# Keys and values formed at the end of the first cross attention, two places that belong to no layer, and a deeper ring for the last gathers

## What is computed

```python
x = x + L0_xattn(layernorm(x), ctx, ctx, mask, ...)   # cross attention to 64 contexts of 257 rows
x = x + L0_attn(layernorm(x), ...)                    # delta rule over chunks, two FIR filters, gated mixture
x = x + L0_ffn(layernorm(x), W1, W2, Wr)              # 8 experts, each row goes to the best 2
x = x + L1_xattn(layernorm(x), ctx, ctx, ...)         # cross attention, 16 heads, the same contexts
x = x + L1_attn(layernorm(x), ...)                    # self attention
x = x + L1_ffn(layernorm(x), ...)                     # 16 experts, best 4, and a shared one
```

```python
k = (K @ Wk.T + bk)      # K = V = ctx: 64 x 257 x 256
v = (V @ Wv.T + bv)
```

## Times and the profile before

| | us |
|---|---|
| median of 3 runs | 1781.69 (1781.23 to 1788.0) |
| the profiled execution | 1793.83 |
| its span | 1792.0 |
| TensorE busy in it | 1591.9 (89%) |
| mean granted TensorE clock in it | 0.941 |

### The profile page before, as it was taken

One profiled execution on the slowest core, in us unless ns is written; L12 is line 12 of the kernel. 1 busy time (PEld: TensorE's weight loads), 2 busy tenths in 40 slices (PEclk: granted clock), 3 DMA queues, 4 the chain that ended last, 5 costly groups with the idle time before them and its releaser, 6 DMA issues. The chain is left out here.

```text
span 1792.0 us, 41190 instructions
## 1 busy us (share of the span) xinstructions
PE 1591.9 (89%) x16490; PEld 1215.2 (68%) x16490; DVE 1211.0 (68%) x2401; ACT 788.2 (44%) x1856; POOL 613.7 (34%) x526
## 2 busy tenths in 40 slices
PE   5986888999988959999999498999989879999998
PEld 3443366555675759999997374566668768689997
DVE  4577889680077448888881316677759867677888
ACT  1222642121133324344442234788827722476664
POOL 2330300000020066666643303587528745203210
PEclk8997989999899969999999798999989979999999
DMA  9990059401043555555538771555500000001001
GB/s 292 321 322 12 1 179 214 128 13 30 2 141 89 153 193 210 204 199 210 193 132 195 188 229 60 184 166 161 168 25 1 1 27 17 13 1 42 24 7 48
DMA packets 143213, 214.84 MB, mean 120 GB/s; under 512 B 38128, under 2 KB 116528, under 8 KB 137136
## 3 DMA queue, kind: packets, MB, share of 16 engines
q1 hardware_dynamic: 106848, 104.06, 20.2%
q0 software_dynamic: 10368, 58.47, 9.8%
q10 hardware_dynamic: 25808, 49.68, 9.5%
HBM read 164.91 MB, written 47.25 MB: 118 GB/s over the span
## 5 line engine op out<-in xcount | busy, mean ns | idle before, releaser
L286 PE MATMUL ps<-kv_ctx,kv_w 128*128 128x257 f32 x512 | 133.1, 396 | 43.2 <-PEq L1824 19.3
L2000 DVE TENSOR_TENSOR f_hL<-f_hr,f_hH 128x512 fp32r<-128x512 f32 x92 | 135.4, 1526 | 46.8 <-ACT f_hH L1951 46.7
L2158 POOL TENSOR_TENSOR a_pr<-a_pr,a_inv 128x1028 f32<-128x1028 f32 x64 | 121.6, 1900 | 72.8 <-DVE a_inv L2278 72.5
L286 PEld LDWEIGHTS ps<-kv_ctx,kv_w 128*128 128x128 f32 x512 | 94.4, 195 | 64.7 <-issue 33.9
L290 PE MATMUL ps<-kv_w,kv_ctx 128*128 128x256 f32 x512 | 124.8, 387 | 13.8 <-ACT b_kv L310 9.3
L96 PE MATMUL ps<-f_xTH,f_w1H 128*128 128x256 f32 x368 | 108.0, 293 | 18.9 <-issue 18.2
L2248 ACT ACTIVATE a_pr<-ps,a_neg 128x257 f32<-128x257 f32 x256 | 117.7, 477 | 2.6 <-DVE a_neg L2298 2.6
L290 PEld LDWEIGHTS ps<-kv_w,kv_ctx 128*128 128x128 f32 x512 | 95.1, 192 | 32.4 <-ACT b_kv L310 13.9
L1512 POOL TENSOR_TENSOR b0m_pm<-b_dr,b_gates 128x256 f32<-128x256 f32 x16 | 13.2, 830 | 296.5 <-SPq L1477 270.1
L97 PE MATMUL ps<-f_xTL,f_w1H 128*128 128x256 f32 x368 | 106.0, 288 | 0.0
L98 PE MATMUL ps<-f_xTH,f_w1L 128*128 128x256 f32 x368 | 105.9, 288 | 0.0
(11 more groups left out here) (421 smaller groups left out, 4532.0 us busy)
## 6 DMA issues: line engine op xcount, KB each, us to landing
a_kv<-kv SPq DMA_DIRECT2D x64, 513.0 KB, 3.6
a_ctxT<-in_ctxT SPq DMA_DIRECT2D x32, 514.0 KB, 7.8
a_ctxR<-in_ctx SPq DMA_DIRECT2D x32, 512.0 KB
kv<-b_kv ACTq DMA_DIRECT2D x31, 513.0 KB, 5.7
kv_ctx<-in_ctxT ACTq DMA_DIRECT2D x61, 257.0 KB, 4.0
kv<-f_raw ACTq DMA_DIRECT2D x15, 513.0 KB, 11.3
outs<-f_yo SPq DMA_DIRECT2D x23, 256.0 KB, 2.1
kv<-f0r_kv ACTq DMA_DIRECT2D x9, 513.0 KB
```

Source lines behind the costliest of these rows:

```text
L286: done = e.matmul(out[:, 0:NK], self.w[:, 0, c, cols(part)], ctx[:, c, :], start=(c == 0), stop=(c == DC - 1))
L2000: e.tensor_tensor(h[1][:, j % 2, 2 * q:2 * q + 2, :], hr[:, q, :, :], h[0][:, j % 2, 2 * q:2 * q + 2, :].bitcast(F32), ALU.subtract).then_ ...
L2158: e.tensor_tensor(pr[:, b % 3, :, :], pr[:, b % 3, :, :], inv[:, b % 2, :].unsqueeze(2).to_broadcast([P, HG, NK]), ALU.mult).then_inc(*p_p ...
```

## The change

**In the first cross attention** two batches (6 jobs) are formed behind the last outputs: TensorE runs them after its loop; ScalarE takes out four jobs ahead of the root of the next layer norm, and two behind it. Of the 64 batches the stages now form 2, 29, 9, 14 and 10. In the delta solve 14 jobs instead of 20 stand ahead of `fuse_most(0)`; the later jobs are at the places where they were, counted from the first.

**Places.** Two places, `A.own`, belong to `KeysAhead` and live through all stages, on the right side of on-chip memory. The wait for a place's store moves into `KvPlace.free`, at its next use; `A.end` is gone. Routing and queries use these two and one of their own, the experts five (two in `raw1`, the two, and one more) instead of three. `xr` is freed after the routing, so GpSimd's first load of expert weights (`gather1(0)`) now stands behind the wait for the stores from it.

**The last gathers** go into 8 places of two (one tile's pair each). A pair waits only from the ninth tile on, until VectorE has used both rows' sums of tile t - 8.

**The root** of the next layer norm at the end of the experts stands behind 36 of 42 evictions; six come after it. With the queries, 12 jobs instead of 9 stand ahead of the query product (`Q.pe`, L346).

```diff
-AHEAD = (31, 9, 15, 9)
+AHEAD = (2, 29, 9, 14, 10)
...
+class KvPlace:
...
+    def free(self, e):
+        if self.used:
+            e.wait_ge(*self.st.at(16 * self.used))
...
+        self.own = [KvPlace(Y, at, f"kv{n}") for n, at in enumerate(places(Y.sb("kv", [P, 2, KV])))]
...
-    def end(self, e):
-        many, count = len(self.kv), (self.last - self.first) // 3
-        for s in range(many):
-            e.wait_ge(*self.st[s].at(16 * ((count - s + many - 1) // many)))
...
+    A.host(AHEAD[0], (6, 7), A.own)
...
+                A.pe(e, 3 * AHEAD[0])
...
+                A.act(e, 3 * AHEAD[0] - 2)
                 K.norms["b0"].act(e)
+                A.act(e, 2)
...
-                ahead.pe(e, 20)
+                ahead.pe(e, 14)
                 fuse_most(0)
...
-                    A.act(e, 3 * AHEAD[1])
-                    A.end(e)
+                    A.act(e, 3 * AHEAD[2])
...
-        A.host(Y, AHEAD[2], (0, 1, 2, 3), places(place1[:, 0:3 * KV].rearrange("p (s n) -> p s n", s=3)))
-        yg = place2[:, 0:4 * D].rearrange("p (s n) -> p s n", s=4)
...
+        A.host(AHEAD[3], (0, 1, 2, 3), [kv2, kv3] + A.own + [kv1])
...
+                e.wait_ge(*st_r.at(16 * NT))
                 gather1(0)
-                e.wait_ge(*st_r.at(16 * NT))
...
-                for n in range(2 * NT):
-                    if n >= 4:
-                        e.wait_ge(*v_x.at(n - 3))
...
+                for t in range(NT):
+                    if t >= RING:
+                        e.wait_ge(*v_x.at(2 * (t - RING) + 2))
+                    for k in range(2):
...
-                A.act(e, 3 * AHEAD[2])
+                A.act(e, 3 * AHEAD[3] - TAIL)
                 K.norms["a1"].act(e)
-                A.end(e)
+                A.act(e, TAIL)
+                for place in (kv1, kv2, kv3):
+                    place.free(e)
...
-                    A.pe(e, 3 * AHEAD[3] - 18)
+                    A.pe(e, 3 * AHEAD[4] - 18)
                     Q.pe(e)
```

More of the change, by code:

```diff
@@ L235, in act, with __init__, store @@
             e.activation(self.raw[:, :], K.ps[:, 2, :], ACT.Copy).then_inc(*self.out.up())
+class KvPlace:
+    def __init__(self, Y, at, name):
+        self.at, self.st, self.used = at, Y.sig("dma", name), 0
+    def free(self, e):
+        if self.used:
+            e.wait_ge(*self.st.at(16 * self.used))
+    def store(self, e, out):
+        e.dma_start(out, self.at).then_inc(*self.st.up(16))
+        self.used += 1
 class KeysAhead:
@@ L252, in __init__, with host, host_of @@
         self.mm, self.ev = Y.sig("pe", "kv"), Y.sig("act", "kv")
-        self.formed = self.taken = self.first = self.last = 0
-    def host(self, Y, count, banks, kv):
-        self.first, self.last = self.last, self.last + 3 * count
-        self.banks, self.kv = banks, kv
-        self.st = [Y.sig("dma", f"kv{s}") for s in range(len(kv))]
+        self.own = [KvPlace(Y, at, f"kv{n}") for n, at in enumerate(places(Y.sb("kv", [P, 2, KV])))]
+        self.formed = self.taken = self.last = 0
+        self.hosts = []
+    def host(self, count, banks, kv):
+        self.hosts.append((self.last, banks, kv))
+        self.last += 3 * count
+    def host_of(self, j):
+        return [h for h in self.hosts if h[0] <= j][-1]
     def load(self, e, b):
@@ L275, in pe @@
             b, part = divmod(j, 3)
-            s, many = b % self.SLOTS, len(self.banks)
-            ctx, out = self.ctx[s], self.K.ps[:, self.banks[(j - self.first) % many], :]
+            first, banks, _ = self.host_of(j)
+            s, many = b % self.SLOTS, len(banks)
+            ctx, out = self.ctx[s], self.K.ps[:, banks[(j - first) % many], :]
             if j == 0:
@@ L302, in act @@
             b, part = divmod(j, 3)
-            own = b - self.first // 3
-            s = own % len(self.kv)
-            kv, src = self.kv[s], self.K.ps[:, self.banks[(j - self.first) % len(self.banks)], :]
+            first, banks, kv = self.host_of(j)
+            place = kv[(b - first // 3) % len(kv)]
+            src = self.K.ps[:, banks[(j - first) % len(banks)], :]
             e.wait_ge(*self.mm.at(j + 1))
-            if part == 0 and own >= len(self.kv):
-                e.wait_ge(*self.st[s].at(16 * (own // len(self.kv))))
+            if part == 0:
+                place.free(e)
             if part < 2:
-                done = e.activation(kv[:, cols(part, NK)], src[:, 0:NK], ACT.Identity, bias=self.bk[:, part:part + 1])
+                done = e.activation(place.at[:, cols(part, NK)], src[:, 0:NK], ACT.Identity, bias=self.bk[:, part:part + 1])
             else:
-                done = e.activation(kv[:, 2 * NK:KV], src, ACT.Copy)
+                done = e.activation(place.at[:, 2 * NK:KV], src, ACT.Copy)
             done.then_inc(*self.ev.up())
@@ L318, in act @@
                 e.wait_ge(*self.ev.at(j + 1))
-                e.dma_start(self.K.kv[b], kv).then_inc(*self.st[s].up(16))
-    def end(self, e):
-        many, count = len(self.kv), (self.last - self.first) // 3
-        for s in range(many):
-            e.wait_ge(*self.st[s].at(16 * ((count - s + many - 1) // many)))
+                place.store(e, self.K.kv[b])
 def places(t):
@@ L915, in delta_attention @@
         A = K.keys
-        A.host(Y, AHEAD[0], (6, 7), places(sb("kv", [P, 2, KV])))
+        A.host(AHEAD[1], (6, 7), A.own)
         with Layer(K, "b0a") as Z:
@@ L1325, in _ @@
                     ahead.act(e, 1)
-                ahead.act(e, 56)
+                ahead.act(e, 50)
                 e.wait_ge(*ld_2.at(96))
@@ L1531, in _ @@
                 K.norms["f0"].act(e)
-                ahead.end(e)
             @block.vector
@@ L1650, in experts_0 @@
             A = K.keys
-            A.host(Z, AHEAD[1], (6, 7), places(Z.sb("kv", [P, 3, KV])))
+            A.host(AHEAD[2], (6, 7), A.own + [kv1])
             T = NormTranspose(Z, rows=xr, logits=(wr, E, rl[:, :, :]))
@@ L1807, in experts_0 @@
         ld_w1, ld_w2 = ([Y.sig("pooldma", f"{n}{s}") for s in range(2)] for n in ("w1", "w2"))
-        ld_g = [Y.sig("pooldma", f"g{s}") for s in range(4)]
+        ld_g = [Y.sig("pooldma", f"g{s}") for s in range(RING)]
         st_y = [Y.sig("dma", f"y{s}") for s in range(2)]
@@ L2047, in cross_attention_1 @@
             A = K.keys
-            A.host(Z, AHEAD[3], (6, 7), places(Z.sb("kv", [P, 3, KV])))
+            kv1 = KvPlace(Z, Z.sb("kv1", [P, KV])[:, :], "kv1")
+            A.host(AHEAD[4], (6, 7), A.own + [kv1])
             ld, d_vl = Z.sigs_of("dma", "w vl")
@@ L2098, in _ @@
                     T.act(e, lambda t: A.act(e, 1))
-                    A.act(e, 3 * AHEAD[3] - 18)
-                    A.end(e)
+                    A.act(e, 3 * AHEAD[4] - 18)
+                    for place in A.own + [kv1]:
+                        place.free(e)
                 @block.gpsimd
```

37 lines of the change are left out of this document (21 added, 16 removed).

## The result

The changed kernel takes 1787.41 us (median of 20 executions, 1777.69 to 1797.12) against 1782.88 us before (20 executions, 1770.88 to 1790.62); the ratio is 1.0034, with a 95% interval of 1.0018 to 1.0051. The forecast was 1759.4. The measured time lies outside the range of 1747 to 1772.

A forecast was written before the change was run, and what follows sets the result against it. Each stage costs what its last engine takes, with DMA bytes pacing the experts' tail; five separate places sum: +1.1 - 8.5 - 1.6 - 16 + 2.7 = -22.3 us from the 1781.7 median, giving 1759.4, range 1747 to 1772.

The forecast's parts named there:

- end of the first cross attention: Two added batches fit TensorE's idle time, but ScalarE's two evictions behind the root end the stage later: +1.1 us.
- delta solve: Six jobs fewer ahead of `fuse_most(0)` start it earlier, and the gain reaches the stage's end: -8.5 us.
- routing to experts: Between these stages, removing `A.end`'s wait for the last store shortens the gap: -1.6 us (0 to -1.7).
- experts' tail: End of the experts: gathers alone no longer trail the last batch, bytes set the pace, root before six evictions: -16 us.
- queries: Start of the queries: one batch more costs 3.6 us, a start nearer full clock saves 1: +2.7 us.
- slower than before: Experts' tail: sixteen scattered gathers drag the DMA rate down, stores hold ScalarE and TensorE; +20 there, 1795 us; chance 0.04.
- a tail that gains less, at 200 GB/s: Experts' tail: the DMA mix runs slower than 222 GB/s, gaining only 7 us; 1768.4 us; chance 0.14.
- a share by turns: Experts' tail: DMA engines alternate between gathers' and ScalarE's queues, four gathers trail the last batch; 1761 us; chance 0.05.
- a start at the full clock: Queries: TensorE, busy until shortly before, begins at full clock or soon gets there: -1 us (0 to -1.9).

The follow-up runs named there:

- no_a0_2: Changed kernel without the two batches in the first cross attention (20 jobs ahead of `fuse_most(0)` as before), on chip 10: 1.0069 of the kernel before.
- a_third: The changed kernel unaltered, run a third time, on chip 10: 1783.57 us median, 1.0051 of the kernel before.
- b_ring8: The kernel before with only the sixteen gather places added (pairs of a tile), batches and root order as before, on chip 15: 1.0064 of before.
- a_fourth: The changed kernel unaltered, run again on chip 9: 0.9886 of the kernel before.
- pace: Changed kernel with an idle GpSimd memset of about 0.7 us behind each last gather, on chip 4: 0.9951 of the kernel before.

## Why the prediction was wrong, point by point

| term | forecast, us | measured, us |
|---|---|---|
| end of the first cross attention | +1.1 | +0.86 (10.51 to 11.37; 11.36 or 11.37 in all but one of the traces with the two batches) |
| delta solve | -8.5 | -7.0 (projections to the last fuse product: 305.6 in the mean of 16 traces, 301.0 to 310.7, against 312.6 in 4 without the move, 311.0 to 316.0) |
| routing to experts | -1.6 | -1.4 |
| experts' tail | -16 | -0.5, +2.2, +0.4 on chips with late updates; -10.2 on chip 9 |
| queries | +2.7 | +4.8 (48.5 in the mean of 18 traces, 44.4 to 51.9, against 43.7 in two) |

**First cross attention: right.** The clock stayed low behind a gap of 3.2 us, as the earlier trace rows had suggested, and ScalarE's two evictions set the end.

**Delta solve: right**, a little less than forecast: `fuse_most(0)` moved up by 9 us in the mean of the traces and the stage kept 7 of them. `no_a0_2` against `a_third` gives 4.7 us for this and the first term together, forecast 7.4.

**Routing: right.** With `A.end` gone the gap is 1.07 or 1.08 us in every trace that has the change, against 2.48 in before and 3.31 in b_ring8. That fits a wait for stores whose landing varies; no run took `A.end` out alone.

**Experts' tail: the step that failed.** The prediction priced GpSimd's issues at 0.94 + 0.30 us each and let them run beside everything at no cost to others; its bounds were bytes, engine time and the share of the queues. That 32 issues without a break could hold up what TensorE and ScalarE tell each other stood in none of its cases. The case "slower than before" had the right place and the right look (sixteen gathers ahead, ScalarE held, TensorE with it), but another mechanism, a mixed DMA rate below 174 GB/s, and it was given 4%. In the trace of before no train was longer than five gathers (the first five, issued from 948.79 to 953.82), so it could not be read there. Instead the tail took 81.4 us, 84.0 and 82.3 on chips 15 and 10, with ScalarE's evictions up to 31 us behind their jobs. Where the lateness is absent, most of the step comes true: 71.7 us on chip 9 with eight pairs, 67.3 with four, against 65.8 forecast (81.8 - 16), and 0.9886 of before is 20.5 us, forecast 22.3; but the terms do not add up to that (below), so the nearness of the two is in part luck. What is left of the miss there is the rate: 15.2 MB in 65.8 us would be 231 GB/s, rows 11 had 222, and over the whole tail a_fourth moved 212 GB/s with the DMA engines 94% busy. In kind that is the prediction's rival of a tail that gains less, at 200 GB/s; in size it lies between the forecast and that rival. The rival of a share by turns, as it was priced (about two gathers for each batch, four left behind the last), has nothing that speaks for it: in those tails 32 gathers are used after 51 to 62 us, before the last batch. How the queues share packet by packet no run shows.

**Queries: the sign was right, the size was not.** The prediction took 1 us off for a start at the full clock. In the first trace that did not come: the first eight records of the stage take 3.77 us behind a gap of 3.97 us, where they took 3.76 behind 19.28 (in a_fourth 3.41 behind 5.55, in pace 1.98 behind 1.55). So the one batch costs nearly its full 3.6 us, and the rest is put down to ScalarE waiting for stores: the two places that belong to no layer are the last that the experts use and the first that the queries use, so their stores, issued in the last 7 us of the tail, have to land first (7.0 us for one). In the experts' end `place.free` for the third last batch costs some 3 us, where the prediction put nothing.

**What stays open.** The terms as measured add up to about -2 us on the chips with late updates; timed it is 0 to +9 us. On chip 9 they add up to some -13, timed -20. Stages that the change does not touch differ by as much between single traces (from the query product's end to the last layer 453 to 462 us, the first stage 141 to 149 us), and of the unchanged kernel there is one trace. So single traces settle terms of this size only where many agree. Why updates come late, and why on some chips only, stays open.

## What to carry to other kernels

A ring that lets GpSimd issue gathers without waiting removes one wait and may create another on engines that have nothing to do with it: look at the waits of ScalarE and TensorE for each other beside such a train. Two things left nothing late on a chip that shows the lateness: 0.7 us of other work behind each gather (one trace, chip 10), and a ring of four places (one trace, chip 15), which however made the gathers the last again. On time alone the changed kernel with `RING = 4` is the one to take: 0.989 of before on chip 15, where eight pairs gave 1.0002, and 0.9887 on chip 9, the same as eight pairs there (0.9886); but its one trace on chip 15 still had late updates. Pauses of 0.7 us gave 0.9951 on chip 4 and 0.9983 on chip 10. When the same code gives a per cent more or less, ask which chip it was on before asking what the edit did: run the version to be judged and its undoing on one chip, and trace both.

## What the hardware showed that I had not expected

TensorE's semaphore updates reached ScalarE up to 31 us late, one every 10 us or so, while GpSimd issued a gather every 1.25 us, on chips 10 and 15 and in the first trace; on chips 4 and 9 the same train made none late. With a gather every 1.9 us none was late on chip 10. In the traces with late updates 453 to 478 of the 512 landing records of the gathers are missing. And TensorE's clock fell in these stalls: 0.63 of full speed in the mean from 946 to 978, and the value job behind the last stall took 3.73 us in place of 1.89.
